# Second cross attention: three PSUM banks for row scores and two for transposed scores, in place of two and three

## The chip, the cores and the metric

The kernel runs on one core of one Trainium2 chip. The metric is device time in microseconds (us). In the profile PE is TensorE's matmuls, PEld its weight loads, DVE is VectorE, ACT is ScalarE, POOL is GpSimd and SP is SyncE, which issues the DMAs. PSUM has eight banks of 128 partitions by 512 fp32 values; matmuls write there, and DVE and ACT read from there.

## What is computed

Two blocks of a gated multimodal transformer, for 4 sequences of 512 tokens with 512 features, with a context of 4 x 512 x 128. Each block is a cross attention and a feed-forward part, both added to `x` through a tanh gate. The change lies in the second cross attention alone:

```
q = rms_norm(layernorm(x)); k = rms_norm(ctx); v = ctx
# 16 query heads of 32, 4 key heads of 32, four query heads share a key head
q = q * cos + rotate_half(q) * sin;  k = k * cos + rotate_half(k) * sin
scores = einsum('bgnqd,bgkd->bgnqk', q, k) / sqrt(32)
scores = where(causal, scores, -1e30)
attn   = softmax(scores)
out    = einsum('bgnqk,bgkd->bgnqd', attn, v) -> (4, 512, 512)
x      = x + tanh(g_xattn[1]) * (out @ w_out.T)
```

The causal mask leaves, for each block of 128 queries, the keys up to the end of that block, and for each block of 128 keys, the queries from its start on.

## The kernel before, in words

The kernel runs in phases, one after the other: first cross attention, first feed-forward part, second cross attention (`xattn1`, from line 1389), second feed-forward part (`ffn1`, from line 2000). In a phase every engine has its own program, and engines wait for each other through semaphores alone. Each engine takes its own instructions strictly in the order in which they are written.

`xattn1` works on 16 groups, each one sequence and one key head with its four query heads. A group is cut into 11 units, so there are 176 units. Each score is computed twice. First **by rows**: `scores(u)` (L1865) puts 128 queries by their keys into one of the `c_s` banks, with fp16 operands of 96 rows (L1875) and a matmul that adds the mask (L1878). DVE takes the row maximum of it in `maximum(u)` (L1660). After the 11 units of a group, `row_parts(G)` on DVE (L1668, L1670) splits the 64 maxima per partition into two fp16 parts, `nparts`. Then PE turns them in `rows(G, 0)` and `rows(G, 1)` (L1891, eight small transposes each) into partitions 96 and 97 of a `c_e` bank, and ACT copies them in `rows_out` (L1765) into two extra rows of the query operand `qaT`. Second, **transposed**: `shifted(u)` (L1894) computes 128 keys by their queries with 98 rows, so that the maximum is already taken off (L1906, and the mask L1908), into a `c_e` bank, and ACT's `exponentials(u)` (L1778) writes the exponentials to `probs` in SBUF. `probs` then goes into fp32 matmuls: `weigh(G, 0..3)` with the values (L1921), and `total(G)` (L1935), the sums of the rows, for which POOL adds two regions beforehand (L1590). DVE inverts the sums (L1677), `expand(G)` (L1943) spreads them over the partitions, DVE multiplies (L1683), and after four groups `project` (L1951) applies the output weights, and DVE adds the residual (L1689).

All engines walk through the same steps `u = 0, 1, 2, ...`. At step u PE does, in this order: `scores(u)`, `shifted(u - 15)`, `rows` (at the steps 11 G + 12 and 11 G + 13 for group G), a `turn` at fixed steps (L1862, which transposes keys or queries of the next sequence into the bank `c_tr`), `weigh`, `total` (at the steps 11 G + 32, which is the last unit of a group), `expand`, `project`. At step u ACT does the exponentials of unit u - 15, `rows_out`, the copy of a finished `c_av` (L1784), the copy of a finished turn (L1759), a part of the next sequence's queries (L441), and then at fixed steps pieces of the next phase's weights: absolute values with their sum (L1788, one step in 6 up to step 82), later scaling (L1795) and storing (L1799). DVE does `maximum(u)`, then `row_parts`, the inverses, and at fixed steps the next sequence's preparation (L344 to L449) and the clipping of weights (L1695).

PE waits for banks in this way. `scores(u)` writes bank u mod 2 and waits until DVE has read unit u - 2. The `c_e` banks are a ring of three that `rows` and `shifted` share; each write is a "fill", numbered in PE's order, and fill f waits until ACT has read fill f - 3. The first `shifted` of a group also waits until its second `rows_out` is done, whatever the banks are. At the two steps with `rows` the order of fills is: exponential block, `rows(G, 0)`, exponential block, `rows(G, 1)`. The eight banks are 2 `c_s`, 3 `c_e`, `c_av`, `c_y` and `c_tr`. Before the steps begin, five turns of the first sequence go out through five banks at once (`early_ps`, L1523), and PE waits until all five are read.

Of the kernel before, what the change touches and what calls it, by code (L numbers as in the profile page):

```python
# [4 lines left out]
P = 128  # L5
# [287 lines left out]
class Preparation:  # L293
# [5 lines left out]
    AUG = SPLITS * HD  # L299
# [1089 lines left out]
def xattn1(nc, a, ph, sb, ps, sem, g):  # L1389
# [48 lines left out]
    s_ps = [ps(f"c_s{k}", [P, SEQ], where=ph) for k in range(2)]  # L1438
    e_ps = [ps(f"c_e{k}", [P, SEQ], where=ph) for k in range(3)]
# [83 lines left out]
    early_ps = [bank[:].bitcast(fp16) for bank in (e_ps[0], e_ps[1], e_ps[2], y_ps, av_ps)]  # L1523
# [3 lines left out]
    with nc.Block() as block:  # L1527
# [95 lines left out]
        def _(dve):  # L1623
# [32 lines left out]
            def maximum(u):  # L1656
                G, r = group(u)
                i, n, heads = QUERY_UNITS[r]
                dve.wait_ge(s_done, u + 1)
                nc.vector.tensor_reduce(nmax[:, G % 2, i, n:n + heads],  # L1660
                                        s_ps[u % 2][:, 0:heads * (i + 1) * P].rearrange("p (n k) -> p n k", n=heads),
                                        axis=AX, op=ALU.max, negate=True).then_inc(max_ready, 1)
# [87 lines left out]
        def _(act):  # L1750
# [10 lines left out]
            def rows_out(G, k):  # L1761
                fill = ROWS_FILL[G, k]
                act.wait_ge(e_done, fill + 1)
                h = G % KV_HEADS * GROUP + 2 * k
                nc.scalar.activation(qaT[AUG:FULL, h:h + 2, :], row_ps[fill % 3][AUG:FULL, :].rearrange("p (h n) -> p h n", h=2),  # L1765
                                     ACT.Copy).then_inc(e_read, 1)

            def exponentials(u):
                G, r = group(u)
                k, n, heads = KEY_UNITS[r]  # L1770
                if r == 0 and G >= 2:
                    act.wait_ge(av_done, G - 1)
                    act.wait_ge(den_done, G - 1)
                fill = EXP_FILL[u]
                act.wait_ge(e_done, fill + 1)
                width = heads * WIDTH[k]
                at = START[k] + n * WIDTH[k]
                nc.scalar.activation(probs[:, G % 2, at:at + width], e_ps[fill % 3][:, 0:width], ACT.Exp).then_inc(e_read, 1)  # L1778
# [59 lines left out]
        def _(pe):  # L1838
# [26 lines left out]
            def scores(u):  # L1865
# [5 lines left out]
                if u >= 2:  # L1871
                    pe.wait_ge(max_ready, u - 1)
                width = (i + 1) * P
                for m in range(heads):
                    nc.tensor.matmul(s_ps[u % 2][:, m * width:(m + 1) * width],  # L1875
                                     qaT[0:AUG, grp * GROUP + n + m, i * P:(i + 1) * P],
                                     kT[0:AUG, b % 2, grp, 0:width], start=True, stop=False)
                    last = nc.tensor.matmul(s_ps[u % 2][:, m * width + i * P:(m + 1) * width], ident_b[:], mask[:],  # L1878
                                            start=False, stop=True)
                last.then_inc(s_done, 1)  # L1880

            def rows(G, k):
# [3 lines left out]
                if fill >= 3:  # L1886
                    pe.wait_ge(e_read, fill - 2)
                for m in range(2):
                    for i in range(TILES):
                        at = m * SEQ + i * P  # L1890
                        last = nc.tensor.transpose(row_ps[fill % 3][AUG:FULL, at:at + P], nparts[:, G % 2, i, 2 * k + m, :], ident_h[:])  # L1891
                last.then_inc(e_done, 1)

            def shifted(u):  # L1894
# [6 lines left out]
                if fill >= 3:  # L1901
                    pe.wait_ge(e_read, fill - 2)
                width = WIDTH[k]
                h = grp * GROUP + n
                for m in range(heads):
                    nc.tensor.matmul(e_ps[fill % 3][:, m * width:(m + 1) * width], kT[0:FULL, b % 2, grp, k * P:(k + 1) * P],  # L1906
                                     qaT[0:FULL, h + m, k * P:], start=True, stop=False)
                    last = nc.tensor.matmul(e_ps[fill % 3][:, m * width:m * width + P], mask[:], ident_b[:],  # L1908
# [406 lines left out]
```

## Time and profile before

| | us |
|---|---|
| median of 3 runs | 837.15 |
| lowest and highest run | 835.89 and 839.64 |
| the profiled execution, its own time | 839.7 |
| its span in the profile | 837.9 |
| TensorE's granted clock over the span | 0.925 |

| engine | busy us | share of the span | instructions |
|---|---|---|---|
| PE | 662.7 | 79% | 5174 |
| DVE | 644.6 | 77% | 978 |
| ACT | 610.9 | 73% | 814 |
| POOL | 383.5 | 46% | 493 |

The span is the time from the first to the last instruction in the profile; 1.8 us of the profiled execution lie around it. Busy times are sums over instructions. Matmuls overlap one another, and their ends are modelled, so that a row of PE that starts before the last one ended is normal; what counts is the time from start to start. The second cross attention runs from the first `scores` at 340.04 us to the last exponential block at 659.14 us, and the fp32 matmuls behind it go on to 668 us.

### The profile page before, as it was taken

What the parts mean: (1) busy time and instruction counts of PE and PEld (TensorE: products, weight loads), DVE (VectorE), ACT (ScalarE), POOL (GpSimd) and SP (SyncE); (2) the same over time, 40 slices, a digit from 0 to 9 for tenths busy, and PEclk for the clock granted to TensorE, in tenths of its full rate; (3) what the DMA queues carried; (4) which work ended last, traced back from release to release, by engine and by line L of the source; (5) the groups of instructions that cost most, each with busy time, mean ns of one, the idle gap of its engine ahead of it and who ended that gap; (6) DMA issues with size and microseconds to landing.
All of it is one profiled execution on the core that took longest, in us unless ns stands there. A gap on an engine that the chain in (4) does not pass through costs nothing. (4 is left out here: it accounts for less than half of the span.)

```text
span 837.9 us, 13670 instructions
## 1 busy us (share of the span) xinstructions
PE 662.7 (79%) x5174; PEld 362.7 (43%) x5174; DVE 644.6 (77%) x978; ACT 610.9 (73%) x814; POOL 383.5 (46%) x493
## 2 busy tenths in 40 slices
PE   8853367876767756679989896989999799888886
PEld 6421123332333323445654564555646444444443
DVE  3689999999999896895885489556635448888884
ACT  3787699989968993488884587658937427767775
POOL 1016526656684775273373148311303416565652
PEclk9996589999979988779999999899999889999999
DMA  8900300000000000622331021112300000100011
GB/s 309 388 2 0 133 18 2 1 0 1 1 0 2 1 0 1 226 70 70 81 120 35 1 70 37 48 40 69 114 1 2 5 31 1 39 26 26 26 38 50
DMA packets 21906, 43.72 MB, mean 52 GB/s; under 512 B 3921, under 2 KB 8529, under 8 KB 21073
## 3 DMA queue, kind: packets, MB, share of 16 engines
q1 hardware_dynamic: 21840, 42.85, 15.0%
q8 instruction: 41, 0.67, 0.3%
q14 instruction: 25, 0.20, 0.1%
HBM read 38.61 MB, written 4.19 MB: 51 GB/s over the span
## 5 line engine op out<-in xcount | busy, mean ns | idle before, releaser
L1660 DVE TENSOR_REDUCE c_nmax<-c_s 128x1 f32<-128x384 f32 (+3 forms) x176 | 108.7, 634 | 83.7 <-PE c_s L1878 83.7
L1778 ACT ACTIVATE c_probs<-c_e 128x512 f32<-128x512 f32 (+1 forms) x176 | 94.6, 559 | 57.7 <-PE c_e L1908 56.7
L1590 POOL TENSOR_TENSOR c_psum<-c_probs 128x1536 f32<-128x1536 f32 x16 | 55.9, 3495 | 156.4 <-ACT c_probs L1778 156.4
L1362 PE MATMUL b_y<-w2q,b_q2T 128*128 128x512 bf16 x256 | 71.8, 433 | 54.5 <-ACT b_q2T L1279 30.1
L2227 PE MATMUL d_gu<-gateq,d_xqT 128*128 128x512 bf16 (+1 forms) x384 | 84.0, 362 | 14.1 <-ACT d_xqT L2152 13.8
L1875 PE MATMUL c_s<-c_kT,c_qaT 96*128 96x128 f16 (+3 forms) x256 | 73.1, 319 | 22.8 <-DVE c_nmax L1660 20.5
L1333 PE MATMUL b_up<-shared,b_xqT 128*128 128x512 bf16 x256 | 70.9, 402 | 2.7 <-ACT hidden L1245 2.7
L1906 PE MATMUL c_e<-c_qaT,c_kT 98*128 98x512 f16 (+3 forms) x256 | 69.8, 307 | 3.4 <-ACT c_qaT L1765 2.8
L1362 PEld LDWEIGHTS b_y<-w2q,b_q2T 128*128 128x128 bf16 x256 | 25.8, 107 | 91.4 <-issue 43.7
L2227 PEld LDWEIGHTS d_gu<-gateq,d_xqT 128*128 128x128 bf16 x384 | 35.1, 98 | 50.4 <-ACT d_xqT L2152 19.8
L1875 PEld LDWEIGHTS c_s<-c_kT,c_qaT 96*128 96x128 f16 x256 | 25.6, 101 | 68.0 <-DVE c_nmax L1660 39.5
L1878 PE MATMUL c_s<-c_mask,ident_b 128*128 128x128 bf16 x256 | 52.9, 231 | 0.0
L1908 PE MATMUL c_e<-ident_b,c_mask 128*128 128x128 bf16 x256 | 50.7, 223 | 0.0
L2066 DVE SCALAR_TENSOR_TENSOR d_h<-d_gu,c_xsin,d_sg 128x512 f32<-128x512 f32 (+1 forms) x48 | 33.7, 702 | 19.6 <-ACT d_sg L2162 19.5
L429 POOL TENSOR_TENSOR c_xsin<-c_xw,ssin 128x256 f32<-128x256 f32 x32 | 33.0, 1050 | 30.4 <-DVE c_xw L413 30.4
L2250 PE MATMUL d_y<-downq,d_q2T 128*128 128x512 bf16 x176 | 40.6, 379 | 4.0 <-ACT d_q2T L2187 4.0
L2162 ACT ACTIVATE d_sg<-d_gu,c_xsin 128x512 f32<-128x512 f32 (+1 forms) x48 | 30.9, 643 | 14.9 <-PE d_gu L2227 14.9
L1333 PEld LDWEIGHTS b_up<-shared,b_xqT 128*128 128x128 bf16 x256 | 25.8, 103 | 33.8 <-issue 10.6
L290 ACT ACTIVATE c_turned<-c_turned,c_xsin 128x512 f32<-128x512 f32 x16 | 11.6, 723 | 39.2 <-POOL c_xsin L283 39.2
L1083 DVE SCALAR_TENSOR_TENSOR b_h<-b_h,b_rstd,b_ln_b 128x2048 f32<-128x2048 f32 x16 | 37.9, 2370 | 1.4 <-POOL b_rstd L1182 1.4
L1075 DVE SCALAR_TENSOR_TENSOR b_h<-hidden,b_nmu,b_ln_g 128x2048 f32<-128x2048 f32 x16 | 38.5, 2407 | 0.0
L1765 ACT ACTIVATE c_qaT<-c_e 2x1024 f16<-2x1024 f16 x32 | 32.5, 1017 | 7.3 <-PE c_e L1891 6.6
(245 smaller groups left out, 1872.2 us busy)
## 6 DMA issues: line engine op xcount, KB each, us to landing
c_stage<-in_gateT SPq DMA_DIRECT2D x16, 704.0 KB, 4.0
c_stage<-in_downT SPq DMA_DIRECT2D x6, 768.0 KB, 4.5
xs<-in_x SPq DMA_DIRECT2D x4, 1024.0 KB, 14.9
a_w1f<-in_w1T SPq DMA_DIRECT2D x2, 2048.0 KB, 16.7
hidden<-in_w2T SPq DMA_DIRECT2D x2, 2048.0 KB, 22.3
out<-xs SPq DMA_DIRECT2D x16, 256.0 KB, 2.0
b_ln_g<-in_ln_g SPq DMA_DIRECT2D x1, 1024.0 KB, 4.8
b_ln_b<-in_ln_b SPq DMA_DIRECT2D x1, 1024.0 KB, 8.5
```

The lines of the kernel that those rows point to most:

```text
L1075: nc.vector.scalar_tensor_tensor(out=h2[:, n % H2S, :], in0=h[:, n % HS, :], scalar=nmu[:, n:n + 1], in1=ln_g[:], op0=ALU.add, op1=ALU.mul ...
L1333: nc.tensor.matmul(up_ps[k][:, m * DIM:(m + 1) * DIM], xqT[:, n % 4, c, :], w1q[:, c, at:at + DIM], start=(c == 0), stop=False)
L1362: last = nc.tensor.matmul(y_ps[:], q2T[:, n % 2, c, :], w2q[:, c, :], start=(c == 0), stop=(c == IC - 1))
L1590: nc.gpsimd.tensor_tensor(psum[:], region(slot, 0)[:, :, P:], region(slot, 1), ALU.add).then_inc(psum_ready, 1)
L1660: nc.vector.tensor_reduce(nmax[:, G % 2, i, n:n + heads], s_ps[u % 2][:, 0:heads * (i + 1) * P].rearrange("p (n k) -> p n k", n=heads), ax ...
L1778: nc.scalar.activation(probs[:, G % 2, at:at + width], e_ps[fill % 3][:, 0:width], ACT.Exp).then_inc(e_read, 1)
L1875: nc.tensor.matmul(s_ps[u % 2][:, m * width:(m + 1) * width], qaT[0:AUG, grp * GROUP + n + m, i * P:(i + 1) * P], kT[0:AUG, b % 2, grp, 0: ...
L1878: last = nc.tensor.matmul(s_ps[u % 2][:, m * width + i * P:(m + 1) * width], ident_b[:], mask[:], start=False, stop=True)
L1906: nc.tensor.matmul(e_ps[fill % 3][:, m * width:(m + 1) * width], kT[0:FULL, b % 2, grp, k * P:(k + 1) * P], qaT[0:FULL, h + m, k * P:], st ...
L1908: last = nc.tensor.matmul(e_ps[fill % 3][:, m * width:m * width + P], mask[:], ident_b[:], start=False, stop=True)
L2227: last = nc.tensor.matmul(gu_ps[part % 2][:, half, 0:WIDTHS[k]], xqT[:, n % 2, c, :], gateq[:, c, at:at + WIDTHS[k]], start=(c == 0), stop ...
L2250: last = nc.tensor.matmul(y_ps[:], q2T[:, n % 2, c, :], downq[:, c, :], start=(c == 0), stop=(c == NC1 - 1))
```

## The change

The row scores get a third bank, and the ring of the transposed scores loses one: 3 + 2 + 3 = 8 banks as before. `scores(u)` waits for the maximum of unit u - 3 in place of u - 2, and fill f waits until ACT has read fill f - 2 in place of f - 3. No instruction is added, removed or moved, and the order on every engine stays. One of the five early turns goes through the new bank, since there is no third `c_e`.

```diff
-    s_ps = [ps(f"c_s{k}", [P, SEQ], where=ph) for k in range(2)]
-    e_ps = [ps(f"c_e{k}", [P, SEQ], where=ph) for k in range(3)]
+    S_BANKS, E_BANKS = 3, 2
+    s_ps = [ps(f"c_s{k}", [P, SEQ], where=ph) for k in range(S_BANKS)]
+    e_ps = [ps(f"c_e{k}", [P, SEQ], where=ph) for k in range(E_BANKS)]
...
-    early_ps = [bank[:].bitcast(fp16) for bank in (e_ps[0], e_ps[1], e_ps[2], y_ps, av_ps)]
+    early_ps = [bank[:].bitcast(fp16) for bank in (e_ps[0], e_ps[1], s_ps[2], y_ps, av_ps)]
...
-                if u >= 2:
-                    pe.wait_ge(max_ready, u - 1)
+                if u >= S_BANKS:
+                    pe.wait_ge(max_ready, u - S_BANKS + 1)
...
-                if fill >= 3:
-                    pe.wait_ge(e_read, fill - 2)
+                if fill >= E_BANKS:
+                    pe.wait_ge(e_read, fill - E_BANKS + 1)
```

The last of these stands in `rows` and in `shifted`; the indices `% 2` and `% 3` of the banks become `% S_BANKS` and `% E_BANKS` in all five places that use them.

## Rows read from the trace of the kernel before

**Rows 1.** Busy time by stretch: us, each engine's busy us (instructions), clock, DMA, GB/s.
```profile
340.00:660.00 320.00, 287.07 (x3110) 171.32 (x3114) 213.62 (x360) 225.82 (x322) 118.71 (x97) 0.95 0.20 62
```

**Rows 2.** Waits, 340 to 660 us: engine, line, for whom: us, times, longest.
```profile
PE c_s L1875 <- DVE c_nmax L1660: 20.5, 21, 2.7
PE c_e L1906 <- ACT c_qaT L1765: 2.8, 5, 1.0
PE c_e L1906 <- ACT c_probs L1778: 0.5, 1, 0.5
...
PEld c_s L1875 <- DVE c_nmax L1660: 39.5, 46, 3.0
```

**Rows 3.** Timeline, group 13's row fills: start, us, instruction, [idle before <-releaser].
```profile
604.04 0.61 PE L1891 MATMUL c_e<-ident_h,c_nparts 128*2 128x128 f16 x8
605.36 0.61 PE L1891 MATMUL c_e<-ident_h,c_nparts 128*2 128x128 f16 x8
...
604.76 1.02 ACT L1765 ACTIVATE c_qaT<-c_e 2x1024 f16<-2x1024 f16 x1
```

**Rows 4.** Timeline, last unit of a group beside a weight piece, step 43.
```profile
399.94 0.33 PE L1906 MATMUL c_e<-c_qaT,c_kT 98*128 98x384 f16 x1
...
399.12 1.37 ACT L1788 ACTIVATE gateq<-c_stage 128x1408 bf16<-128x1408 f32 x1
...
400.48 0.48 ACT L1778 ACTIVATE c_probs<-c_e 128x384 f32<-128x384 f32 x1
```

**Rows 5.** Timeline, group 10's row fills and the score block behind them.
```profile
558.27 0.61 PE L1891 MATMUL c_e<-ident_h,c_nparts 128*2 128x128 f16 x8 [0.42 <-ACT c_probs L1778]
...
558.24 1.02 ACT L1765 ACTIVATE c_qaT<-c_e 2x1024 f16<-2x1024 f16 x1
...
561.30 0.34 PE L1875 MATMUL c_s<-c_kT,c_qaT 96*128 96x384 f16 x1 [0.21 <-DVE c_nmax L1660]
```

**Rows 6.** Timeline, first exponential block of group 8.
```profile
506.69 0.39 PE L1906 MATMUL c_e<-c_qaT,c_kT 98*128 98x512 f16 x1 [1.03 <-ACT c_qaT L1765]
```

**Rows 7.** Timeline, score blocks that waited for DVE, and what follows two of them.
```profile
496.80 0.39 PE L1875 MATMUL c_s<-c_kT,c_qaT 96*128 96x512 f16 x1 [0.46 <-DVE c_nmax L1660]
...
497.99 0.39 PE L1875 MATMUL c_s<-c_kT,c_qaT 96*128 96x512 f16 x1 [0.52 <-DVE c_nmax L1660]
...
500.45 0.18 DVE L1670 TENSOR_TENSOR c_nparts<-c_nmax,c_nparts 128x16 f16<-128x16 f32 x1
...
501.73 0.61 PE L1891 MATMUL c_e<-ident_h,c_nparts 128*2 128x128 f16 x8
...
600.24 0.39 PE L1875 MATMUL c_s<-c_kT,c_qaT 96*128 96x512 f16 x1 [0.62 <-DVE c_nmax L1660]
```

**Rows 8.** Timeline, 429.7 to 438 us, while DVE prepares a sequence.
```profile
432.50 0.39 PE L1875 MATMUL c_s<-c_kT,c_qaT 96*128 96x512 f16 x1 [2.73 <-DVE c_nmax L1660]
...
437.45 0.18 DVE L1670 TENSOR_TENSOR c_nparts<-c_nmax,c_nparts 128x16 f16<-128x16 f32 x1
...
437.84 0.61 PE L1891 MATMUL c_e<-ident_h,c_nparts 128*2 128x128 f16 x8
```

**Rows 9.** Busy time of stretches at the ends of DVE's preparations.
```profile
429.70:432.50 2.80, 0.07 (x3) 0.01 (x1) 2.73 (x6) 2.80 (x5) 1.31 (x2) 1.00 0.00 0
432.50:436.40 3.90, 3.90 (x61) 2.86 (x62) 3.87 (x5) 2.69 (x4) 3.19 (x3) 0.56 0.41 118
436.40:439.70 3.30, 3.30 (x46) 2.60 (x43) 3.23 (x7) 2.19 (x4) 2.27 (x3) 1.00 0.48 165
...
360.00:380.00 20.00, 13.75 (x112) 8.17 (x113) 17.71 (x25) 17.96 (x26) 16.48 (x13) 0.74 0.23 73
...
522.10:528.90 6.80, 6.74 (x48) 5.32 (x49) 6.54 (x11) 4.82 (x6) 3.85 (x4) 0.54 0.00 1
```

**Rows 10.** Timeline near the end: unit 171 on PE, units 168 and 169 on ACT.
```profile
654.29 0.33 PE L1906 MATMUL c_e<-c_qaT,c_kT 98*128 98x384 f16 x1
...
653.58 1.17 ACT L1778 ACTIVATE c_probs<-c_e 128x512 f32<-128x512 f32 x2 [0.35 <-PE c_e L1908]
```

More of the change, by code:

```diff
@@ L1764, in rows_out @@
                 h = G % KV_HEADS * GROUP + 2 * k
-                nc.scalar.activation(qaT[AUG:FULL, h:h + 2, :], row_ps[fill % 3][AUG:FULL, :].rearrange("p (h n) -> p h n", h=2),
+                nc.scalar.activation(qaT[AUG:FULL, h:h + 2, :], row_ps[fill % E_BANKS][AUG:FULL, :].rearrange("p (h n) -> p h n", h=2),
                                      ACT.Copy).then_inc(e_read, 1)
@@ L1777, in exponentials @@
                 at = START[k] + n * WIDTH[k]
-                nc.scalar.activation(probs[:, G % 2, at:at + width], e_ps[fill % 3][:, 0:width], ACT.Exp).then_inc(e_read, 1)
+                nc.scalar.activation(probs[:, G % 2, at:at + width], e_ps[fill % E_BANKS][:, 0:width], ACT.Exp).then_inc(e_read, 1)
             def weighed_out(G):
@@ L1870, in scores @@
                     pe.wait_ge(tr_read, TURNED_FOR(G))
-                if u >= 2:
-                    pe.wait_ge(max_ready, u - 1)
+                if u >= S_BANKS:
+                    pe.wait_ge(max_ready, u - S_BANKS + 1)
                 width = (i + 1) * P
                 for m in range(heads):
-                    nc.tensor.matmul(s_ps[u % 2][:, m * width:(m + 1) * width],
+                    nc.tensor.matmul(s_ps[u % S_BANKS][:, m * width:(m + 1) * width],
                                      qaT[0:AUG, grp * GROUP + n + m, i * P:(i + 1) * P],
                                      kT[0:AUG, b % 2, grp, 0:width], start=True, stop=False)
-                    last = nc.tensor.matmul(s_ps[u % 2][:, m * width + i * P:(m + 1) * width], ident_b[:], mask[:],
+                    last = nc.tensor.matmul(s_ps[u % S_BANKS][:, m * width + i * P:(m + 1) * width], ident_b[:], mask[:],
                                             start=False, stop=True)
@@ L1890, in rows @@
                         at = m * SEQ + i * P
-                        last = nc.tensor.transpose(row_ps[fill % 3][AUG:FULL, at:at + P], nparts[:, G % 2, i, 2 * k + m, :], ident_h[:])
+                        last = nc.tensor.transpose(row_ps[fill % E_BANKS][AUG:FULL, at:at + P], nparts[:, G % 2, i, 2 * k + m, :], ident_h[:])
                 last.then_inc(e_done, 1)
@@ L1900, in shifted @@
                     pe.wait_ge(e_read, ROWS_FILL[G, 1] + 1)
-                if fill >= 3:
-                    pe.wait_ge(e_read, fill - 2)
+                if fill >= E_BANKS:
+                    pe.wait_ge(e_read, fill - E_BANKS + 1)
                 width = WIDTH[k]
@@ L1905, in shifted @@
                 for m in range(heads):
-                    nc.tensor.matmul(e_ps[fill % 3][:, m * width:(m + 1) * width], kT[0:FULL, b % 2, grp, k * P:(k + 1) * P],
+                    nc.tensor.matmul(e_ps[fill % E_BANKS][:, m * width:(m + 1) * width], kT[0:FULL, b % 2, grp, k * P:(k + 1) * P],
                                      qaT[0:FULL, h + m, k * P:], start=True, stop=False)
-                    last = nc.tensor.matmul(e_ps[fill % 3][:, m * width:m * width + P], mask[:], ident_b[:],
+                    last = nc.tensor.matmul(e_ps[fill % E_BANKS][:, m * width:m * width + P], mask[:], ident_b[:],
                                             start=False, stop=True)
```

2 lines of the change are left out of this document (1 added, 1 removed).

## The prediction, made before the changed kernel ran

> **What bounds the kernel now.** I read the phase of the change alone, first by stretch, then the waits, then the timeline around each wait for a bank. Over 340 to 660 us PE is busy for 287 of 320 us, ACT for 226, DVE for 214 [rows 1]. So PE's order of work sets the time of most of the phase, and a stall of PE counts unless something late ends the stretch anyway. PE waits 20.5 us, 21 times, for row maxima in front of score blocks; counted at its weight loads it is 39.5 us, 46 times. For the ring of transposed scores it waits 0.5 us once, and 2.8 us for the rows copied by ACT, a wait on data, not on a bank [rows 2]. At first sight the change gives a bank to the side that waits and takes it from one that never does. Two questions decide: how many of the 20.5 us come back, and where two `c_e` banks are too few.
>
> I answered both by setting, for every unit and fill, PE's start against the end of the read that the new wait names. In this trace PE starts 0.06 us after the end of a read that it waited for. A score block is freed if unit u - 3 was read; a fill is late by what is missing between its start and the end of the read of fill f - 2, plus 0.06. I then went through the phase in order, and carried PE's shift along, since a delay uncovers one stall and covers the next.
>
> **Gains at the row scores.** Five stalls of 2.1 to 2.9 us and nine small ones at the start fall in stretches in which DVE prepares the next sequence without a pause, as from 429.7 us on. PE waits 2.7 us there, then works, and `rows(5, 0)` starts at 437.84, 0.2 us after the parts of the maxima are ready at 437.63 [rows 8]. With a third bank PE passes the score block at once, runs ahead by a step, and stands at the same `rows`, for DVE's chain is as long as before. It regains 0.14 us there, nothing in the stretch that ends at 523.5 us, where the same margin is 0.08 us, and 0.3 us up to 379 us, where ACT's chain starts from the same parts. Sum 0.4 us, out of some 20 us of stalls as they stand from start to start.
>
> What PE does regain are the short stalls outside these stretches, at the last units of a group: 0.78 us at 600.24 (idle by the row 0.62; the start comes 0.78 later than PE's usual distance, since modelled ends hide the rest), and in the same form 0.51 at 415.3, 0.24 at 508.3, and 0.22 each at 481.5 and 643.2. The two at 496.80 and 497.99 are 1.3 us together, but DVE has no pause there and finishes the parts at 500.63, and `rows(8, 0)` starts at 501.73, so at most 1.04 us [rows 7]. Sum 3.0 us. Others, at 383.9, 399.7, 561.3, 568.6, 571.2 and 585.1, are taken over by a new wait right behind them, below. Gains together: 3.4 us.
>
> **Costs at the ring.** (a) In every group but the first, `rows(G, 1)` is fill f, and fill f - 2 is `rows(G, 0)`, with one exponential block between. ACT reads `rows(G, 0)` from 604.76 to 605.78; PE starts `rows(G, 1)` at 605.36 and would have to wait until 605.84 [rows 3]. That is 0.48 us, in the same form in groups 4, 6, 13 and 14, where PE is the bound: 1.9 us. In groups 1, 3, 7 and 9 a turn of PE lies between, and the read is over in time: nothing. In groups 2 and 8 (and 11) ACT is behind with a weight piece and PE stands before the first exponential block of the next group for some time anyway, in group 8 for 1.03 us [rows 6]; the 0.5 to 0.85 us fit in there: nothing. Group 5 is in a stretch of DVE: nothing beyond the above. Group 10: the read of `rows(10, 0)` ends at 559.26, and `rows(10, 1)` starts at 558.27, so +1.04, of which the stall of 0.37 at 561.30 (0.21 by the row) is no longer needed: +0.67 [rows 5]. Group 12: +0.37, as ACT's delay there is partly used up by (b). Group 15: the read of `rows(15, 0)` starts late, +0.54. Sum of (a): 3.5 us.
>
> (b) At three group ends a weight piece of 1.4 to 1.6 us on ACT meets three exponential blocks that PE issues within 1.3 us. At 399.94 PE fills a bank whose predecessor but one is read from 400.48 to 400.96: it would start at 401.02, +1.08 [rows 4]. The same happens at 585.4, +0.98, and at 568.9, +1.08, of which 0.33 come back at the score stall at 571.20: +0.75. Behind the waiting block in PE's queue is `total(G)`, and then the next scores, for which DVE and ACT both wait. No slack: 2.8 us.
>
> (c) At 654.29 PE fills a bank whose predecessor but one ACT reads until 654.75: +0.52 [rows 10]. `total(14)` is behind it, DVE's inverse behind that, and behind it DVE's chain into the next phase.
>
> Costs together 3.5 + 2.8 + 0.5 = 6.8 us, gains 3.4 us: **+3.4 us**. The phases behind only start later by that. The profiled execution took 839.7 us and would take 843.1; it lies 2.5 us over the median, and the sum is a difference, so for the median 837.15 + 3.4 = 840.6 us. Bounds of the single terms: every short score stall gives all it shows and (a) is absorbed wherever ACT is behind, about 0; every late fill of (a) and (b) at its full size, about +6.
>
> The early turn through the third score bank costs nothing: PE waits for all five reads before the steps begin, and these are the same reads.
>
> **The rivals.**
> The clock (slower): PE's idle time in the three stretches of DVE comes in one piece. Now it is 2.8 us idle at full clock, after which the next 3.9 us run at a granted clock of 0.56, and the 3.3 us behind again at 1.00, where `rows(5, 0)` begins [rows 9]. With the third bank the first stall goes, PE does the work up to `rows`, and then stands for about 4.5 us before 437.7. If the clock falls to its lower level (1.2 GHz) only then, it falls on the work that the end of the stretch depends on: 3.3 us of PE between 437.8 and 441.1, most of it at half speed, of which ACT's chain covers a part. Price about 2 us a stretch, in the two later ones, the second by a longer low clock: 840.6 + 4 = 844.6 us. Against it: at the end of the other two stretches the clock is low already, 0.74 over 360 to 380 us and 0.54 over 522.1 to 528.9 [rows 9]. It decides if the clock is under 1.00 just after `rows(5, 0)`.
> The Trainium skill, "TensorE: Matmul & The Clock Gate", section "What's actually happening", says that the throttled state is the default and that activity lifts it; the trace agrees that the clock falls around idle time and recovers under work, and the page leaves open on which matmuls it falls here.
>
> All late fills add up (slower): 37 fills are late by 18.2 us in all, each taken alone; less 3.7 us it is 851.6 us. It needs that ACT's reads move with PE. Against it, ACT's reads behind a weight piece do not depend on PE, and PE waits there already [rows 6].
>
> The stalls come back (faster): if DVE's preparation happens to fall better, or PE's lead outlives `rows`, a good part of the 20.5 us comes back. With one step of PE, 1.4 us, in each of the three stretches, and half of (a) absorbed: 3.4 - 4.2 - 1.7 = -2.5, 834.6 us; with all 20.5 us less 6.8, 823.5 us. Against it: the 0.2 us before `rows(5, 0)` [rows 8].
> The Trainium skill, "Perfetto Trace Analysis", section "Identifying Performance Opportunities", says that the same gap repeating on the engine that should be busy can mean too little PSUM for the next tile; by it the change should bring the faster outcome. The gaps repeat as it says, but they come while DVE has no pause, which no bank alters.
>
> Nothing (same): gains and costs cancel, or DVE's pauses take up both: 837.2 us.
>
> **How the numbers follow.** The forecast, 840.6 us with a range of its own of 837.5 to 843.5, 0.63; the clock, 0.15; all late fills, 0.06; faster, 0.07; nothing, 0.09. The range of 8 in 10 takes in the forecast's, the clock's, and the zero: 836.0 to 845.5 us. A measurement can tell about 0.5% from no change, here 4.2 us. The forecast's sum is under that, but near: 0.38 of its 0.63 lies beyond, which is 0.24; with 0.13 of the clock and 0.06 it is 0.43 slower, 0.05 faster, and 0.52 the same.
>
> **What would show it.** In the profile of the changed kernel: the wait of `scores` for maxima goes to few cases; PE waits for ACT's read of `rows(G, 0)` in front of `rows(G, 1)`, about 0.5 us in groups 4, 6, 13 and 14, and for exponentials at the ends of three groups, about 1 us; PE stands for over 4 us before `rows(5, 0)` and `rows(9, 0)`, which start after DVE's parts as now; the phase takes about 3.4 us longer. If the first `rows` after a preparation start earlier, the faster rival holds; if the clock is low behind them, the clock's. The prediction is wrong if ACT's order or durations move by over 1 us, since most terms are that small.

## The result, and the profile after

The change made the kernel slower by about 1%. In runs side by side the median was 845.07 us (844.55 to 845.84, 5 runs) against 835.92 us (835.81 to 839.64, 5 runs) before, a ratio of 1.0099 [1.0085, 1.0112], which is +8.3 us on 837.15. The forecast was 840.6 us, +3.4 us; the time lies inside the range of 836.0 to 845.5 us, near its upper end, and above the 837.5 to 843.5 us that the sum had for itself.

One execution of each was profiled, 845.07 us after and 839.7 us before. Their spans differ by only 5.4 us, because the phases ahead of the change, which it does not touch, happened to be 1.5 us shorter in the profile after: the first `scores` starts at 338.51 us there and at 340.04 before. So I read the loss inside the phase, from the first `scores` to the start of `total(15)` on PE: 321.18 us before, 328.38 after, **+7.2 us**. That is the number which the terms of the prediction have to explain. Behind the phase the two profiles agree within 0.4 us. In the code after, line numbers are higher by one than in the rows of before (scores L1876, row maxima L1661, `rows` L1892, transposed scores L1907, `rows_out` L1766, exponentials L1779, clip L1696, POOL's sum L1591).

The waits after, 340 to 668 us (engine, line, for whom: us in total, times, longest), which answer to [rows 2]:

```profile
PEld c_s L1876 <- DVE c_nmax L1661: 19.3, 29, 1.7
...
PE c_e L1892 <- DVE c_nparts L1671: 12.7, 4, 5.3
...
PEld c_e L1907 <- ACT c_probs L1779: 10.9, 15, 1.5
...
PEld c_e L1892 <- ACT c_qaT L1766: 7.6, 13, 0.9
...
PE c_s L1876 <- DVE c_nmax L1661: 6.5, 7, 1.6
...
PE c_e L1907 <- ACT c_probs L1779: 5.7, 9, 1.1
...
PE c_e L1892 <- ACT c_qaT L1766: 4.4, 11, 0.7
```

The third score bank does what it says: PE's wait for maxima falls from 20.5 us to 6.5 us. But 12.7 us stand now in front of four `rows`, for DVE's parts, and 10.1 us (5.7 and 4.4) are waits for ACT's reads of the ring, where there were 0.9: the 0.5 of [rows 2], and 0.42 at 558.27 us [rows 5], a row fill, which [rows 2] does not have. The sum of PE's waits did not fall: 23.8 us before [rows 2], 29.3 us in the PE rows here.

The busy time of the same stretch, which answers to [rows 1]:

```profile
340.00:660.00 320.00, 279.89 (x2999) 166.24 (x2998) 212.76 (x354) 222.75 (x316) 114.87 (x96) 0.95 0.18 60
```

In a window of the same length PE is busy 7.2 us less, at the same mean clock of 0.95: it gets through less of the same work (2999 matmuls against 3110) and stands more. That the difference is the same number as the 7.2 us of the phase is chance, for the windows cut the phase at different points.

To see where, I set each unit's `scores` in both profiles against the first one of its own profile. The shift (after less before, us) by unit:

| unit | 27 | 44 | 60 | 71 | 82 | 98 | 104 | 116 | 121 | 132 | 142 | 148 | 160 | 169 | `total(15)` |
|---|---|---|---|---|---|---|---|---|---|---|---|---|---|---|---|
| shift | -0.29 | 0.87 | 0.83 | 1.23 | 1.70 | 0.50 | 0.39 | 1.52 | 1.52 | 2.92 | 2.78 | 5.31 | 5.77 | 6.25 | 7.21 |

The loss comes in small steps over the whole phase. The two usual steps look like this after. First group 13's `rows`, the stretch of [rows 3], on PE and on ACT:

```profile
607.87 0.61 PE L1892 MATMUL c_e<-ident_h,c_nparts 128*2 128x128 f16 x8
...
609.61 0.61 PE L1892 MATMUL c_e<-ident_h,c_nparts 128*2 128x128 f16 x8 [0.34 <-ACT c_qaT L1766]
...
608.54 1.02 ACT L1766 ACTIVATE c_qaT<-c_e 2x1024 f16<-2x1024 f16 x1
```

From start to start the two `rows` are 1.74 us apart, 1.32 before; `rows(13, 1)` starts 0.05 us after ACT's read ended at 609.56. Second, step 43, the stretch of [rows 4]:

```profile
399.27 0.34 PE L1907 MATMUL c_e<-c_qaT,c_kT 98*128 98x384 f16 x1 [1.14 <-ACT c_probs L1779]
...
397.38 1.37 ACT L1789 ACTIVATE gateq<-c_stage 128x1408 bf16<-128x1408 f32 x1
398.64 0.20 ACT L1789 ACTIVATION_READ_ACCUMULATOR gateq<-c_stage 128x1 f32 x1
398.74 0.48 ACT L1779 ACTIVATE c_probs<-c_e 128x384 f32<-128x384 f32 x1
```

The weight piece holds ACT, the bank's last reader but one is queued behind it, and PE stands for 1.14 us.

### The profile page after: what moved, and what is told of

The parts are those of the page before. It is cut to its first block and busy times, and to the rows that moved or that the text cites. A ratio compares the mean times of both kernels' runs of the same rounds, so it can differ in the third digit from the quotient of the medians.

```text
span 843.3 us, 13670 instructions
## 1 busy us (share of the span) xinstructions
PE 662.0 (79%) x5174; PEld 361.7 (43%) x5174; DVE 647.7 (77%) x978; ACT 610.9 (72%) x814; POOL 378.6 (45%) x493
## 5 line engine op out<-in xcount | busy, mean ns | idle before, releaser
L1661 DVE TENSOR_REDUCE c_nmax<-c_s 128x1 f32<-128x384 f32 (+3 forms) x176 | 108.1, 632 | 88.3 <-PE c_s L1879 88.1
L1779 ACT ACTIVATE c_probs<-c_e 128x512 f32<-128x512 f32 (+1 forms) x176 | 94.5, 557 | 57.8 <-PE c_e L1909 56.5
L1591 POOL TENSOR_TENSOR c_psum<-c_probs 128x1536 f32<-128x1536 f32 x16 | 55.0, 3440 | 164.2 <-ACT c_probs L1779 164.2
L1362 PE MATMUL b_y<-w2q,b_q2T 128*128 128x512 bf16 x256 | 74.3, 444 | 52.5 <-ACT b_q2T L1279 29.4
L1876 PE MATMUL c_s<-c_kT,c_qaT 96*128 96x128 f16 (+3 forms) x256 | 72.6, 317 | 8.5 <-DVE c_nmax L1661 6.5
L1907 PE MATMUL c_e<-c_qaT,c_kT 98*128 98x512 f16 (+3 forms) x256 | 69.8, 306 | 6.8 <-ACT c_probs L1779 5.7
L1876 PEld LDWEIGHTS c_s<-c_kT,c_qaT 96*128 96x128 f16 x256 | 25.6, 101 | 50.0 <-issue 24.7
L1766 ACT ACTIVATE c_qaT<-c_e 2x1024 f16<-2x1024 f16 x32 | 32.5, 1016 | 12.9 <-PE c_e L1892 11.8
## 6 DMA issues: line engine op xcount, KB each, us to landing
xs<-in_x SPq DMA_DIRECT2D x4, 1024.0 KB, 14.5
```

The source lines that it names most:

```text
L1362: last = nc.tensor.matmul(y_ps[:], q2T[:, n % 2, c, :], w2q[:, c, :], start=(c == 0), stop=(c == IC - 1))
L1591: nc.gpsimd.tensor_tensor(psum[:], region(slot, 0)[:, :, P:], region(slot, 1), ALU.add).then_inc(psum_ready, 1)
L1661: nc.vector.tensor_reduce(nmax[:, G % 2, i, n:n + heads], s_ps[u % S_BANKS][:, 0:heads * (i + 1) * P].rearrange("p (n k) -> p n k", n=head ...
L1876: nc.tensor.matmul(s_ps[u % S_BANKS][:, m * width:(m + 1) * width], qaT[0:AUG, grp * GROUP + n + m, i * P:(i + 1) * P], kT[0:AUG, b % 2, g ...
L1907: nc.tensor.matmul(e_ps[fill % E_BANKS][:, m * width:(m + 1) * width], kT[0:FULL, b % 2, grp, k * P:(k + 1) * P], qaT[0:FULL, h + m, k * P ...
```

## The experiments

For each variant the ratio to the kernel before was taken from runs side by side. The medians of before in the three sets were 837.13, 837.11 and 837.36 us. "Phase" is the length from the first `scores` to `total(15)` in the variant's own profile (before 321.18 us, after 328.38 us). A "difference by the ratios" is the difference of two ratios times 837 us; its 95% interval is about 2 to 3 us to either side (1 to 2 us for a single ratio).

How far a phase length can be trusted shows at unit 27. Up to there four of the profiled kernels (the one before, short clips, idle matmuls and late clips before) have the same instructions, and yet their `scores(27)` stand at 0, +0.56, -0.77 and +0.71 us in the count of the shift table. So a difference of two phase lengths holds 1 us or more of chance. Up to 375 us the clock changes its level several times, and not at the same work in each profile. Growth between two later units is read more safely.

| variant | median us | ratio [95%] | phase us |
|---|---|---|---|
| score banks 2, ring 2 | 845.08 | 1.0095 [1.0079, 1.0111] | 329.54 |
| `c_y` given up: 2, 3 | 872.47 | 1.0425 [1.0401, 1.0448] | 358.85 |
| `c_y` given up: 3, 3 | 872.60 | 1.0416 [1.0392, 1.0440] | 357.24 |
| `c_y` given up: 3, 2 | 879.11 | 1.0505 [1.0487, 1.0523] | 364.28 |
| half `rows_out`, 3 and 2 | 841.82 | 1.0055 [1.0041, 1.0069] | 323.64 |
| half `rows_out`, before | 836.52 | 0.9990 [0.9974, 1.0005] | 320.16 |
| short clips, 3 and 2 | 841.32 | 1.0049 [1.0031, 1.0066] | 325.55 |
| short clips, before | 834.52 | 0.9966 [0.9952, 0.9979] | 319.05 |
| idle matmuls, 3 and 2 | 849.96 | 1.0166 [1.0135, 1.0197] | 333.67 |
| idle matmuls, before | 837.32 | 1.0004 [0.9992, 1.0017] | 319.63 |
| two late clips, before | 836.96 | 1.0002 [0.9986, 1.0017] | 320.88 |
| two late clips, 3 and 2 | 842.71 | 1.0066 [1.0049, 1.0084] | 327.74 |

### Each bank by itself

The first question is which half of the change costs, and whether the other half gives anything. Two banks for each can be had by leaving one unused:

```diff
-    S_BANKS, E_BANKS = 3, 2
+    S_BANKS, E_BANKS = 2, 2
```

> Two banks for row scores and two for the transposed ones; one bank of PSUM stays unused, so that only the ring's loss is made. Theory A (the ring of two costs all of the loss, and the third score bank gives back a few short stalls): 8 to 11 us over the kernel before, which is 0 to 3 us more than the changed kernel. Theory B (the third score bank is itself harmful, as PE's lead gathers its idle time in one piece and shifts PE's work against DVE's): 4 to 7 us over the kernel before, less than the changed kernel. In the trace, score stalls as before the change, and PE in front of the second row fill as in the changed kernel.

Measured: 1.0095, +8.0 us, and +8.4 us in the phase. The ring's bank is the whole loss. The changed kernel, which has a score bank more than this one, is 1.2 us shorter in the phase and the same by the runs (1.0099 against 1.0095). Of the 1.2 us, 1.0 stands already at unit 27 (-0.29 against +0.67), within the chance named above; from there to `total(15)` the two differ by 0.2 us. The waits of this kernel over the same stretch:

```profile
PE c_s L1876 <- DVE c_nmax L1661: 19.7, 20, 2.7
...
PE c_e L1907 <- ACT c_probs L1779: 5.4, 9, 1.1
PE c_e L1892 <- ACT c_qaT L1766: 4.7, 12, 0.7
```

With two score banks PE waits 19.7 us for maxima, with three 6.5 us. Removing 13 us of this wait was worth 1.2 us at most.

The same two questions can be put the other way, with three banks on both sides. For that a bank has to come from elsewhere; here `c_y` is given up, and `expand` and `project` share `c_tr` with the turns and totals, which costs a lot by itself:

```diff
-    av_ps, y_ps = ps("c_av", [P, SEQ], where=ph), ps("c_y", [P, SEQ], where=ph)
+    av_ps = ps("c_av", [P, SEQ], where=ph)
...
-    out_ps = [y_ps[:], den_ps, y_ps[:], den_ps]
+    out_ps = [den_ps] * 4
...
-                take("y", attn_ready, G + 1)
+                take("tr", attn_ready, G + 1)
...
-                take(("y", "tr")[i % 2], y_read, b * TILES + i + 1)
+                take("tr", y_read, b * TILES + i + 1)
```

> The bank c_y is given up: expand and project go through the bank of the turns. Banks 2 and 3 as before. It frees a bank, so that with the next two the score bank and the ring's bank can be changed one at a time. New waits between turns, expand and project: 10 to 30 us over the kernel before. It is the base of the next two.

> As e2_shared_s2e3 with three score banks and three in the ring, so only the third score bank is added. Theory A: 1 to 4 us faster than e2_shared_s2e3, for PE waits in the long stretches for DVE's maxima however many score banks there are. The rival that the gaps of PE before score blocks come back as time: 10 us or more faster.

> As e3_shared_s3e3 with two in the ring, so only the ring loses a bank. Theory A: 6 to 11 us slower than e3_shared_s3e3. If the loss of the change has another cause than the ring (the clock, DVE's collisions with POOL), under 4 us.

Giving up `c_y` cost 35 us, more than the 10 to 30 expected. Measured, against each other: the third score bank alone takes 1.6 us off the phase (358.85 to 357.24), 0.8 of it by unit 27, and nothing that the runs can tell (1.0425 to 1.0416); the loss of the ring's third bank adds 7.0 us in the phase and 7.5 us by the ratios (1.0416 to 1.0505). Both agree with the kernel of two and two, in a setting whose other waits are quite different. The waits of the kernel with three and three, 340 to 700 us, show where the score bank's gain goes even when nothing is taken from the ring:

```profile
PE c_e L1892 <- DVE c_nparts L1671: 13.0, 4, 5.2
...
PE c_s L1876 <- DVE c_nmax L1661: 5.8, 5, 2.5
```

PE stands for DVE's parts in front of `rows` in place of standing for DVE's maxima in front of `scores`. In the kernel with two score banks and three in the ring the same two waits are 0.5 and 18.3 us. DVE is late in both.

### The second `rows` behind ACT's long copy

Term (a) of the prediction says that `rows(G, 1)` waits for the 1.02 us that ACT needs to copy `rows(G, 0)`. Here the first copy of each group takes one head of the two, which halves its length, in the changed kernel and in the one before:

```diff
+                if k == 0:
+                    nc.scalar.activation(qaT[AUG:FULL, h, :], row_ps[fill % E_BANKS][AUG:FULL, 0:SEQ], ACT.Copy).then_inc(e_read, 1)
+                    return
```

> The changed kernel with ACT's copy of the first row fill of each group cut to its first head of two (about 0.55 us in place of 1.02; the second head's two extra rows stay zero, so part of the shift by the maximum is left out). Theory A1: rows(G, 1) waits for this read in groups 4, 5, 6, 10, 12 to 15, and that is about 3.5 us of the change's 8.3; with the read short the wait falls from 0.48 to under 0.1 us, and this kernel stays 3.5 to 6 us over e6_half_rows_before. If that wait is hidden elsewhere and the loss comes from the rest, it stays 7 to 9 us over it.

> The kernel before with the same cut of the copy; the base of e5_half_rows_s3e2. Both theories: 0 to 3 us faster than the kernel before, since its PE never waits for the first copy but stands a few times before the first exponential block of a group, for the second copy, which comes earlier too.

Measured: the difference between the two falls from 7.2 to 3.5 us in the phase, and by the ratios from 8.3 to 5.4 us (1.0055 less 0.9990). Group 13 in the changed kernel with the short copy:

```profile
606.60 0.61 PE L1900 MATMUL c_e<-ident_h,c_nparts 128*2 128x128 f16 x8
607.92 0.61 PE L1900 MATMUL c_e<-ident_h,c_nparts 128*2 128x128 f16 x8
...
607.26 0.59 ACT L1772 ACTIVATE c_qaT<-c_e 2x512 f16<-2x512 f16 x1
```

The read ends at 607.85 and the second `rows` starts 0.07 us later, 1.32 us after the first, as before the change: a read of 0.59 us just fits, one of 1.02 us does not. PE's wait for `rows_out` in front of `rows` is 0.2 us once, in place of 4.4 us 11 times. The single steps go too: between units 55 and 60 the shift grows by 0.06 in place of 0.47, between 154 and 160 by 0.07 in place of 0.46, between 160 and 169 by 0.06 in place of 0.48. These steps are sound: 0.4 us each in groups 4, 6, 13 and 14, which the prediction had at 0.48.

The total is less so. 3.7 us in the phase and 2.9 by the ratios are near the 3.5 of term (a), but other things fell into them. The kernel before with the short copy stands at -1.25 at unit 27, and loses 0.78 us between units 60 and 71, where its clock is low from 430.4 to 437.2 us. And in the changed kernel with the short copy, DVE's clip at 504.79 us takes 0.93 us in place of 3.90 (next section), while the growth between units 98 and 116, less that of its base, comes out 2.3 us smaller than with the full copy. So what is shown is that the single waits go with the copy's length; the size of (a) as a whole agrees with 3.5 us and is not measured by it.

### DVE's clip beside POOL's sum

Comparing DVE in both profiles, I found one instruction whose length had changed: the clip of a weight chunk (L1695 before, L1696 after). First around 504 us, before and then after:

```profile
505.00 2.78 DVE L1695 TENSOR_SCALAR c_stage<-c_stage 128x1408 f32<-128x1408 f32 x1 [1.38 <-ACT c_stage L1795]
...
503.58 3.46 POOL L1590 TENSOR_TENSOR c_psum<-c_probs 128x1536 f32<-128x1536 f32 x1
```

```profile
504.03 3.90 DVE L1696 TENSOR_SCALAR c_stage<-c_stage 128x1408 f32<-128x1408 f32 x1 [0.65 <-ACT c_stage L1796]
...
503.74 3.45 POOL L1591 TENSOR_TENSOR c_psum<-c_probs 128x1536 f32<-128x1536 f32 x1
```

In both the clip ends 0.74 us after POOL's sum, which is near the 0.89 us that a clip of this size takes when it is alone. Counted from each profile's first `scores`, the sum starts 1.69 us later after the change and the clip only 0.56 us later, so the clip stands longer beside it. This comes from the third score bank and not from the ring: the clip takes 3.89 to 3.91 us in the kernels with three score banks, also with three in the ring, and 2.76 to 2.78 us in those with two (of those with full copies and with the clips whole and in their place). Then around 590 us, before and then after:

```profile
589.49 0.90 DVE L1695 TENSOR_SCALAR c_stage<-c_stage 128x1536 f32<-128x1536 f32 x1
...
589.44 4.25 POOL L1590 TENSOR_TENSOR c_psum<-c_probs 128x1536 f32<-128x1536 f32 x1 [13.35 <-ACT c_probs L1778]
```

```profile
591.96 3.56 DVE L1696 TENSOR_SCALAR c_stage<-c_stage 128x1536 f32<-128x1536 f32 x1
...
591.27 3.43 POOL L1591 TENSOR_TENSOR c_psum<-c_probs 128x1536 f32<-128x1536 f32 x1 [13.79 <-ACT c_probs L1779]
```

Before, the two start within 0.05 us, the clip takes 0.90 us and POOL's sum 4.25 us, 0.8 longer than usual. After, POOL's sum starts 0.69 us ahead, takes its 3.43 us, and the clip takes 3.56 us. One of the two does its work after the other, and the change decided which. Here it is the ring that decides: the clip at this place has to wait for the sum in all seven profiled kernels with two ring banks, and goes first in all seven with three. To price it, the clips were cut to eight columns in both kernels:

```diff
-                nc.vector.tensor_scalar(chunk, chunk, MAGIC + 1.0, MAGIC - 1.0, ALU.min, ALU.max).then_inc(clipped, 1)
+                nc.vector.tensor_scalar(chunk[:, 0:8], chunk[:, 0:8], MAGIC + 1.0, MAGIC - 1.0, ALU.min, ALU.max).then_inc(clipped, 1)
```

> The changed kernel with DVE's clipping of weight pieces in this phase cut to 8 of up to 1536 columns (the rest of the weights stays unclipped). Theory A2: about 2 us of the change's loss come from two clips that now meet POOL's sum of the exponentials and take 3.9 and 3.6 us, where they took 2.8 and 0.9; so this kernel is 5 to 7 us over e8_short_clip_before. If the longer clips are hidden: 8 us or more over it.

> The kernel before with the same cut of the clips; the base of e7_short_clip_s3e2. 1 to 4 us faster than the kernel before, as DVE has 0.8 us less per piece, 11 times, of which PE's score stalls show a part.

What this edit does has to be read first. It takes the clip's own work away, not its wait for POOL. The clips of eight columns at the two places, in the changed kernel, and the second one before:

```profile
504.49 2.39 DVE L1696 TENSOR_SCALAR c_stage<-c_stage 128x8 f32<-128x8 f32 x1 [1.37 <-ACT c_stage L1796]
...
503.40 3.45 POOL L1591 TENSOR_TENSOR c_psum<-c_probs 128x1536 f32<-128x1536 f32 x1
...
590.66 2.78 DVE L1696 TENSOR_SCALAR c_stage<-c_stage 128x8 f32<-128x8 f32 x1
```

```profile
586.44 0.11 DVE L1695 TENSOR_SCALAR c_stage<-c_stage 128x8 f32<-128x8 f32 x1
```

A clip of eight columns takes 2.39 and 2.78 us where the sum has begun, and ends 0.03 us after it; at 586.44 us it takes 0.11. That one operation stands still for the other is shown by this more clearly than by the whole clips. But the collisions that were to be priced are still in the changed kernel.

Measured: the kernel before gains 2.1 us in the phase, the changed one 2.8 us. The difference is 6.5 us in the phase, 0.7 less than with the clips; by the ratios it is 6.9 us. That is inside what was expected of theory A2, and does not decide for it: the 8 us of its rival lie within the interval, and 0.5 of the 0.7 us stand already at unit 27, long before the first clip at step 87. The growth of the shift by stretch, after less before, with the clips whole, short, and (below) late:

| units | clips whole | clips short | two clips late |
|---|---|---|---|
| 104 to 116 | +1.13 | +0.24 | +0.35 |
| 121 to 132 | +1.40 | +2.12 | +1.80 |
| 142 to 148 | +2.53 | +1.75 | +2.54 |
| 82 to `total(15)` | +5.51 | +5.40 | +5.41 |
| whole phase | 7.20 | 6.49 | 6.85 |

With short clips the shift grows by 0.9 us less around group 9 and by 0.8 us less around group 12. The 0.8 us are the clip's own work (2.78 us against 3.56): DVE sets the time there in the changed kernel. What its wait for the sum costs at this place no run shows, for it was in every kernel with two ring banks. Between units 121 and 132 the kernel before gains 0.7 us by the short clips and the changed one nothing, and that takes most of it back. From unit 82, ahead of the first clip, to the end of the phase the difference is 5.5 us with the clips whole and 5.4 with them short or late: a price read at a place was not found again in the sum.

The milder edit delays two of the clips by two steps, those of the steps 101 and 122, which land beside POOL's sums of groups 7 and 9, at 504 and 557 us. The one at 590 us stays:

```diff
-                if r == 1 and 0 <= q < NP:
+                if r == (3 if q in (2, 5) else 1) and 0 <= q < NP:
```

> The kernel before with the clips of two weight pieces two steps later, past POOL's sum of exponentials. If DVE's clip waits for POOL's instruction and that delays the stretch that ends at 523.5 us: the clip of 2.8 us takes about 0.9, and the kernel is 1 to 2 us faster than before. If the time of the clip is hidden: within 0.5 us.

> The changed kernel with the same two clips two steps later. If the clip of 3.9 us is what moved the stretch before rows(9, 0) by 1.1 us, it is 1.5 to 3 us faster than the changed kernel, and rows(9, 0) starts earlier by as much; if not, within 0.5 us of it.

Measured: nothing in the kernel before (1.0002, -0.3 us in the phase), where 1 to 2 us, or less than 0.5, had been expected. In the changed kernel 0.65 us in the phase, made of -0.97 between units 109 and 116 and +0.41 around unit 70, where the clock was low from 434.6 to 441.5 us; by the ratio it is 2.8 us less than the change (1.0066 against 1.0099, whose intervals do not meet, though the changed kernel was not run again in this set), which the profile does not show. The 1.5 us or more that the theory asked for are in the ratio and not in the profile. At its place the edit works: between DVE's parts of group 8 and of group 9 the shift falls by 1.11 us, where it falls by 0.14 without it; in the kernel before, the same edit makes it fall by 0.43. The moved clip still takes 1.87 us there, for it catches the end of POOL's sum:

```profile
506.00 1.87 DVE L1696 TENSOR_SCALAR c_stage<-c_stage 128x1408 f32<-128x1408 f32 x1
```

### The clock behind the long pause

Around 440 us the event of the clock's rival had come. PE's timeline after, which answers to [rows 8]:

```profile
433.68 0.22 PE L1909 MATMUL c_e<-ident_b,c_mask 128*128 128x128 bf16 x1
437.01 0.61 PE L1892 MATMUL c_e<-ident_h,c_nparts 128*2 128x128 f16 x8 [3.11 <-DVE c_nparts L1671]
...
438.72 1.01 PE L1892 MATMUL c_e<-ident_h,c_nparts 128*2 128x128 f16 x8 [0.32 <-ACT c_qaT L1766]
439.67 1.09 PE L1863 MATMUL c_tr<-ident_h,shared 128*96 128x128 f16 x8
440.55 1.69 PE L1944 MATMUL c_y<-shared,c_chosen 128*128 128x128 f32 x8
442.07 0.33 PE L1876 MATMUL c_s<-c_kT,c_qaT 96*128 96x384 f16 x1
```

And the busy time of three stretches around it, which answer to [rows 9]:

```profile
433.00:438.30 5.30, 1.91 (x22) 1.27 (x20) 5.20 (x8) 2.99 (x5) 4.37 (x4) 1.00 0.62 190
438.30:441.70 3.40, 3.08 (x23) 2.76 (x22) 3.37 (x7) 3.30 (x5) 1.93 (x2) 0.50 0.01 2
441.70:445.10 3.40, 3.40 (x38) 2.15 (x37) 2.62 (x5) 2.98 (x5) 3.37 (x2) 0.99 0.00 0
```

PE's pause is one piece, as the prediction said, though of 3.1 us and not of over 4 (5.3 us in front of `rows(9, 0)`). The granted clock falls to 0.50 (1.2 GHz) not in it but 1.3 us after PE has begun again, and stays there for 3.4 us, over `rows(5, 1)`, a turn and an `expand` that take 1.01, 1.09 and 1.69 us, where they took 0.61, 0.65 and 1.11 before. To take the low clock away, PE was kept busy with matmuls that nothing reads, in groups 5 and 9 of the changed kernel and at the same places before:

```diff
+            def warm(bank, fill, back, u, times):
+                if fill >= back:
+                    pe.wait_ge(e_read, fill - back + 1)
...
+                for _ in range(times):
+                    nc.tensor.matmul(bank[:], qaT[0:AUG, grp * GROUP, 0:P], kT[0:AUG, b % 2, grp, 0:SEQ], start=True, stop=True)
```

> The changed kernel with idle matmuls (14 of 512 columns in group 5, 22 in group 9) into the bank of rows(G, 0), in the stretch in which PE stands for DVE's maxima; the transposes then overwrite them. Clock theory: the granted clock stays at 1.00 from 430 to 460 us and 505 to 535 us, and 1 to 2.5 us of the change's loss go, against the changed kernel. If the clock costs nothing here, since DVE and ACT set the end of these stretches: within 0.5 us of the changed kernel.

> The kernel before with idle matmuls (11 each) in front of the three long score stalls of units 65, 109 and 111, into the ring's next bank. Both theories: the low clock at 432.8 us goes; DVE's chain sets the end of the stretch, so within 1 us of the kernel before. With e9 it tells whether the clock's price belongs to the change or to the kernel.

Measured, before: 1.0004, the same, with no low clock left between 375 and 665 us. So the low clock in the kernel before costs nothing that can be measured, as expected. In the changed kernel the experiment spoiled itself (1.0166, 5.6 us over the change by the ratios):

```profile
436.68 3.19 PE L1871 MATMUL c_e<-c_kT,c_qaT 96*128 96x512 f16 x14 [1.76 <-ACT c_probs L1779]
439.81 0.61 PE L1901 MATMUL c_e<-ident_h,c_nparts 128*2 128x128 f16 x8
```

The idle matmuls write into the bank that `rows` uses next, so they had to wait for ACT's read of it, started late and ran on until 439.8 us, 2.0 us past DVE's parts, which were ready at 437.82. In group 9 it was worse, `rows(9, 0)` at 530.10 against 523.54, and the clock was low there all the same, from 521.0 to 527.8 us. What can still be read is what follows: at the full clock PE needs 3.7 us from `rows(5, 0)` to the scores of unit 69, and 5.1 us in the changed kernel (437.01 to 442.07). So the low clock costs PE 1.4 us there, of which 0.6 are left at unit 71 (7.8 us from `rows(5, 0)` against 7.2). How much of it reaches the end is not shown by a run of its own. The stretch came out 0.54 us over the forecast, but PE's wait of 0.32 us for ACT's copy falls in it too, and the size changes from profile to profile: in the changed kernel with late clips, which is the same up to there, the shift grows by 0.81 us in place of 0.40 between units 60 and 71, and with two and two banks, whose clock is not low between 372.5 and 515.9 us, it falls by 0.55.

## Why the prediction was right in sign and too small

The step of the prediction that was mis-sized is the gains: 3.4 us were booked, and the phase shows few of them kept. One cost, at group 12, was too small as well. Each term of the sum, as forecast and as the shift table (with the units between its columns) has it:

| place | forecast us | seen us |
|---|---|---|
| start, up to 379 us | -0.3 | -0.29 |
| step 43 | +1.08 | +1.08 |
| 415.3 us | -0.51 | -0.51 |
| `rows` of group 4 | +0.48 | +0.47 |
| before `rows(5, 0)` and behind it | -0.14 | **+0.40** |
| `rows` of group 6 | +0.48 | +0.47 |
| 481.5 us | -0.22 | -0.22, lost again by unit 93 |
| 496.8 and 498.0 us | -1.04 | -1.20 |
| group 8, 508.3 us | -0.24 | -0.11 |
| DVE's stretch up to 523.5 us | 0 | **+1.13** |
| `rows` of group 10 | +0.67 | +0.65 |
| 568.9 us | +0.75 | some +0.75 |
| 585.4 us | +0.98 | +1.2 |
| `rows` of group 12 and behind | +0.37 | **+1.31** |
| 600.24 us | -0.78 | **0** |
| `rows` of groups 13 and 14 | +0.48 each | +0.46 and +0.48 |
| 643.2 us | -0.22 | -0.23 |
| `rows` of group 15 | +0.54 | +0.6 |
| 654.29 us | +0.52 | +0.5 |

**The costs were right up to one.** The single steps of 0.48 in term (a) came out at 0.46 to 0.48, and went with the copy's length. The three group ends (b) and the last one (c) came as said, to about 0.2 us. The -0.29 at the start is not a confirmation of the -0.3, since kernels with the same instructions up to there lie up to 1.5 us apart. Comparing a start with the end of the read that the new wait names, for every fill, was a sound way to price a ring that gets shorter.

**The gains were not.** I booked 3.4 us, and the score bank alone gave 1.2 and 1.6 us in two settings, of which 0.2 and 0.8 lie behind unit 27. The four bold rows, and the 0.22 of unit 93 and 0.13 of group 8 that did not stay, make 3.7 us, and 3.4 + 3.7 is the 7.1 of the 7.2 us seen. Apart from the 0.94 us of group 12, a cost, they have one thing in common: each gain was PE's, and another engine or bank behind it had not moved, or not for good.

The gain of 1.04 us at 496.8 and 498.0 came in full, and unit 98 stands at +0.50 after +1.70. DVE took part in it for a while. Counted from the first `scores`, its parts of group 8 are 1.69 us later than before, but its clip at 504 us starts only 0.56 us later. The clip then ends with POOL's sum, which is 1.69 us later, and the parts of group 9 are 1.55 later (at 523.49 against 523.47 us of each profile). `rows(9, 0)` waits for the latter, and the gain ends there. I had costed this stretch at nothing because PE's margin before `rows` was small on both sides. I had not asked by how much DVE's own chain, which began with what PE had lost up to unit 82, would be late at its end. The clip beside the sum is a part of the answer: moved two steps away from it, the parts of group 9 come 0.97 us earlier against those of group 8, 0.54 us more than the same edit gives in the kernel before. That it accounts for the whole stretch is not shown.

In group 12 an order turned. PE's new wait of term (b), 1.05 us at 587.82, came as forecast, and `scores(143)` behind it starts at 589.81 us where it was 587.34, 2.47 us later. POOL's sum waits for the exponentials of unit 128 and starts only 1.83 us later (591.27 against 589.44). So DVE's clip, which hangs on the maximum of unit 143, came 0.69 us after the sum had begun in place of 0.05, and had to let it pass. DVE was 2.7 us busy longer with it, and PE waited for the maxima, with three banks:

```profile
596.17 0.34 PE L1876 MATMUL c_s<-c_kT,c_qaT 96*128 96x384 f16 x1 [0.71 <-DVE c_nmax L1661]
```

The wait of 0.41 us in front of `rows(12, 1)` came too, as forecast, but at 593.07 us, behind the turn. With short clips the clip is 0.78 us shorter and 0.78 us of the loss are gone; the wait for the sum stays, and no run without it was made, so the 0.94 us over the forecast are put down to it by argument. The prediction counted the operations as of fixed length; two that exclude each other are not.

At 600.24 us the score stall is gone as said, [rows 7], and nothing is gained, because `total(11)` behind it now waits for its bank:

```profile
604.67 0.43 PE L1936 MATMUL c_tr<-c_probs,shared 128*32 128x128 f32 x8 [0.77 <-ACT c_qaT L1760]
...
603.59 1.03 ACT L1760 ACTIVATE c_qaT<-c_tr 96x1024 f16<-96x1024 f16 x1
```

Before, `total(11)` began at 600.90, 0.05 us after the same copy had ended at 600.85. It was a wait that was just met, and so did not show. I had carried the shift along, "since a delay uncovers one stall and covers the next", only for the banks `c_s` and `c_e`, not for `c_tr`.

Behind `rows(5, 0)` the prediction had the right event in the wrong case. The clock's rival said that the clock would be under 1.00 just after it, and it was, in one of the two stretches named; its price was to be 2 us, and the stretch came out 0.54 us over the forecast with everything in it. In the other stretch the clock was low before as well as after, as the argument against the rival said.

**The rivals.** The faster one is refuted: the stalls moved to `rows` and did not come back, with three banks in the ring (three and three) too. The Trainium skill, "Perfetto Trace Analysis", section "Identifying Performance Opportunities", says that a repeating gap can mean too little PSUM; here the gap was 20.5 us, and one bank against it was worth 1.6 us of the phase at most. "All late fills add up" had +14.5 us and was too much (counted again from the trace it is 31 fills, by 18.3 us in all). The nearest price was the clock's, 844.6 us, and how much of the loss its mechanism gave is open. That the time lies inside the stated range is so in part by luck: the range reached up to 845.5 for the sake of that rival, and the sum's own ended at 843.5. It should have been wider on the side of loss alone: the costs at the ring came where the rows had a start before the end of a read and PE was the bound, while every gain had to pass all the engines behind it.

**What stays open.** By the runs the change costs 8.3 us, by the profiles 7.2 us in the phase; about 1 us is between one profiled execution and the medians. How much of the 0.54 us behind `rows(5, 0)` is the clock, what the turned order of clip and sum costs at group 12, and why the late clips give more by the ratio than in the profile, was not settled. No variant that does the whole work was faster than the kernel before by more than its interval.

## What to carry to other kernels

Before giving a bank to the side that waits, look at whether the engine it waits for ever pauses: if it does not, the bank only moves the wait to the next place where its result is needed. Before taking one from a side that never waits, compare each start with the end of the read that the shorter ring will name; waits that are just met do not show in the list of waits, and here they were most of the cost. Before counting on an edit that takes something away, look in its profile whether it is gone. A gain on one engine counts only where each engine and bank behind it has that much slack too, and an operation that shares something with another engine has no fixed length.

## What the runs showed of the hardware

A DVE clip of 128 x 1408 or 128 x 1536 fp32 values took 0.90 us when it started with POOL's sum, which then took 4.25 us in place of 3.45, and 2.76 to 3.91 us when the sum had run for 0.3 to 1.4 us before it, and then ended 0.74 to 0.82 us after the sum in each case. A clip of eight columns took 0.11 us in the first case, and 2.04 to 2.78 us in the second, with its end 0.03 us after the sum's. They did not slow each other in part; one did its work after the other. The Trainium skill, "SBUF — State Buffer", section "Who interferes with whom", says that a VectorE operation in a two-port mode and a GpSimd operation lock the shared port pair and that the one that issues second is fully blocked. The trace agrees in the lengths; in which mode the clip ran no row shows. In the case at 589.4 us the profile has POOL's start 0.05 us ahead of DVE's although POOL gave way, and the page's rule of the order can't be told from a row as close as that.

PE's clock fell 1.3 us after work had begun again, not in the pause of over 3 us ahead of it, and it came back after 3.4 us. In the kernel before a low stretch of the same 3.4 us came 5.5 us earlier by the profiles' times, just behind a pause of 2.8 us. Removing it there changed nothing that could be measured (1.0004 [0.9992, 1.0017]).
